# Mixer masks taken in pairs of groups, an fp32 output projection moved by seven steps, and the MLP's transposes one token tile later

## The chip, the cores and the metric

One core of one Trainium2 chip runs the whole program in one launch. The metric is the device time of a launch in microseconds (us), lower is better. TensorE (PE; PEld is its weight load), VectorE (DVE), ScalarE (ACT), GpSimd (POOL) and SyncE (SP, which issues the DMAs) each run their own queue in order and meet at semaphores only.

## The reference, cut to what matters

The input x is 8 sequences x 1024 tokens x 256 features. Three stages follow one another: a Mamba-2 mixer, an MLP (together the "attention" half of a modulated block), and a feed-forward network that the change does not touch.

```
h  = layernorm(x) * (1 + ca) + sa
xn = layernorm(h) * ln_w + ln_b
z, xBC, dt = split(xn @ in_proj_w);  dt = softplus(dt + dt_bias)
x_, B, C   = split(silu(causal_conv1d(xBC)))          # 32 heads of 16, state size 128
state_t = exp(dt*A) * state_(t-1) + dt*x_t (outer) B_t;   y_t = C_t . state_t + D*x_t
y  = y * silu(z)
y  = y * rsqrt(mean(y*y) + 1e-5) * rms_w
o1 = y @ out_proj_w + h                               # mixer
x1 = x + ga * (o1 + relu(layernorm(o1) @ m1 + b1) @ m2 + b2)   # MLP
x  = x1 + gb * feed_forward(layernorm(x1) * (1 + cb) + sb)
```

## The kernel before, in words

**Blocks, chunks, steps.** The mixer works in 16 blocks of 512 tokens, each of 4 chunks of 128 tokens. The scan inside a chunk is a masked product: for every head a 128x128 matrix exp(decay from token s to token t), times the product of B and C (gm), times x. The 32 heads go in 8 groups of 4, so a chunk has 8 steps i = 0..7 and a block 32 steps n = 0..31. Each engine's program is one loop over all steps S = 8q + i (q the chunk); "n" counts from a block's first chunk. While the chunks of one block are scanned, the next block's input side (transposes, input projection, convolution, softplus chain, layer norms) is spread over the same 32 steps by hand: the constants at lines 136 to 156 name the step of each part.

**What a group passes through.** In step S, PE makes group S's decay exponents in a PSUM bank (`decay`, L658), ACT takes exp into a buffer mh (`exponent`, L803), and DVE multiplies the 512 columns by gm (`masked`, L1094). PE uses the result LAG = 5 steps later (`intra`, L672): four fp32 products of 128x32 weights with 128 columns, each placed on 32 of the array's columns by `tile_position`. Heads 2k and 2k+1 add into the same 32 rows of PSUM, so a group of four consecutive heads uses two of the four column tiles, two heads each. There are MH = 7 buffers mh.

**The end of a chunk Q.** DVE's `addends` (step 8Q+9) waits for the last `intra` (PE, step 8Q+12), adds the skip term (L1104) and forms the state's part (yoff_s, L1112). POOL's `gated` (step 8Q+10) adds the two (L907) and multiplies by silu(z) (L914) into yg. ACT (step 8Q+17) makes yh, yg rounded to fp32r (L865), and the square ysq (L866); POOL (step 8Q+16) makes the rest yl = yg - yh (`y_low`, L918). PE (`project`, step 8Q+23) forms yh*wout0 + yh*wout1 + yl*wout0 in twelve one-pass fp32r products of 256 columns (L691, recorded at L645), then the sum of squares with a one-column product (L695). DVE takes the mean (`square_mean`, step 8Q+21, L1119), POOL the power -1/2 (L899), and DVE scales and adds the residual (`residual`, step 8Q+22, L1127). The engines are several steps apart, so such numbers order the work of one engine; they are not times.

**The state.** In i = 1 PE reads the old state (`from_state`, L703), in i = 2 it makes the chunk's contribution (`to_state`, L709, one fp32 product of 512 columns); DVE's `new_state` (i = 0 of the next chunk, L1140 and L1143) waits for it.

**Rings and queues.** PSUM banks are handed round in two rings of three, in the orders that `act_bank_order` and `dve_bank_order` write out (a slot is free again three keys later). SP's queue sends the decay rows (`decay_left`, `decay_right`), stores each finished block (o1) after its last `residual`, and loads the next one.

**The MLP.** 16 blocks of 512 tokens. PE makes eight hidden tiles (m = 0..7), then the second product for the four token tiles c = 0..3: first over the hidden parts k = 0..5 for all c (18 products of 256 columns per c), then k = 6, 7. The transposes of the next block's normalised input go in between (L1310, called at L1346): half k = 0 after c = 0 and half k = 1 after c = 1. They share one PSUM bank: the second waits until ACT has read the first (L1357, L1358). DVE normalises the next block (L1411) after hidden part m = 7, and makes the low part of the transposed input (L1417), with which the next block's products start.

## Time and profile before

| | before |
|---|---|
| median of 3 runs | 3296.01 us (3295.22 to 3304.86) |
| profiled execution | 3288.03 us, span of its instructions 3286.2 us |
| mean granted TensorE clock | 0.941 of 2.4 GHz |
| busy over the span | PE 88%, PEld 67%, DVE 61%, ACT 38%, POOL 24% |
| stages by the trace | set-up to 137 us, mixer to 1421, change of stage to 1449, MLP to 1892, feed-forward to the end |

The busy shares are means over three stages with different limits, so each stage is read by itself: first its busy times by window, then the groups of instructions with the idle time before them and what ended it, then the timeline where the waits lie. A group's "mean ns" is the length of a record; matmuls overlap, so the time that one costs is the distance from its start to the next one's. PE's fp32 products appear as two records each, the one-pass products as one.

### The profile page before, as it was taken

To read this page: it belongs to the slowest core of one execution; us is meant where nothing else is said; L and a number is where in the kernel's file an instruction comes from. 1 tells how busy PE (TensorE), PEld (TensorE's weight loads), DVE (VectorE), ACT (ScalarE), POOL (GpSimd) and SP (SyncE) were. 2 spreads that over 40 slices of the span, in tenths; PEclk is the share of its full clock that TensorE was granted. 3 is DMA by queue.
4 is the path that set the end of the run, shared out by engine and by line. 5 is a ranking of instruction groups with operands and counts; after the bars stand their busy time and mean duration, and the time that the engine had idled before them with its cause. 6 is when DMAs were issued, how large, how long until landed. Compare 5 with 4: busy or idle time off the path is not lost. (4 is left out here: it accounts for less than half of the span.)

```text
span 3286.2 us, 46643 instructions
## 1 busy us (share of the span) xinstructions
PE 2893.6 (88%) x17254; PEld 2215.8 (67%) x17254; DVE 2002.8 (61%) x3954; ACT 1257.5 (38%) x1978; POOL 782.2 (24%) x748
## 2 busy tenths in 40 slices
PE   0588888888888888969988979999999999999999
PEld 0355555555555555558877868787878787878787
DVE  5799989999999999855666533333333333333333
ACT  0455555555555555534555422222222222222221
POOL 5033233333333333320000022222222222222222
PEclk6799989999998999989989989999999999999999
DMA  3000101010101010034211100000000000000000
GB/s 121 28 27 19 34 19 34 20 34 20 34 19 34 19 34 10 28 106 176 73 62 60 47 21 14 16 13 16 13 16 13 15 14 15 13 16 13 15 10 11
DMA packets 104860, 107.11 MB, mean 33 GB/s; under 512 B 35896, under 2 KB 98616, under 8 KB 102976
## 3 DMA queue, kind: packets, MB, share of 16 engines
q1 hardware_dynamic: 99520, 103.81, 9.7%
q8 instruction: 159, 2.61, 0.3%
q10 hardware_dynamic: 5120, 0.19, 0.1%
q14 instruction: 61, 0.50, 0.0%
HBM read 71.41 MB, written 40.94 MB: 34 GB/s over the span
## 5 line engine op out<-in xcount | busy, mean ns | idle before, releaser
L1575 PE MATMUL fbank<-hid,fw 128*128 128x512 f32 x4096 | 962.3, 395 | 0.0
L1575 PEld LDWEIGHTS fbank<-hid,fw 128*128 128x128 f32 x4096 | 765.7, 187 | 187.4
L1725 DVE TENSOR_TENSOR hid<-fhf,hid 128x512 fp32r<-128x512 f32 x384 | 265.4, 691 | 704.4 <-POOL hid L1682 704.4
L803 ACT ACTIVATE mh<-ebank 128x512 f32<-128x512 f32 x512 | 302.8, 601 | 587.9 <-PE ebank L658 587.1
L1682 POOL TENSOR_SCALAR hid<-fhf 128x512 fp32r<-128x512 f32 x384 | 270.6, 705 | 1044.3 <-ACT fhf L1654 760.7
L672 PE MATMUL yin<-mh,xpad 128*32 128x128 f32 x4096 | 345.6, 291 | 104.0 <-DVE mh L1094 102.9
L1094 DVE SCALAR_TENSOR_TENSOR mh<-mh,gm 128x512 f32<-128x512 f32 x512 | 397.0, 782 | 3.1 <-ACT mh L803 3.0
L672 PEld LDWEIGHTS yin<-mh,xpad 128*32 128x32 f32 x4096 | 198.1, 113 | 269.1 <-DVE mh L1094 146.4
L645 PE MATMUL ebank<-ah,win 128*128 128x512 f32 x640 | 246.5, 425 | 6.7 <-DVE al L988 3.6
L1042 DVE SCALAR_TENSOR_TENSOR xc<-cin,cw,xc 128x512 f32<-128x512 f32 x288 | 240.9, 837 | 0.3
L1654 ACT ACTIVATE fhf<-fbank,sh2c 128x512 f32<-128x512 f32 x128 | 88.0, 687 | 382.5 <-PE fbank L1575 382.5
L1598 PE MATMUL fbank<-fah,fw 128*128 128x512 f32 x512 | 205.1, 401 | 16.3 <-issue 12.5
L658 PE MATMUL ebank<-cright,cleft 102*128 102x512 bf16 x512 | 208.2, 407 | 8.6 <-ACT ecs L858 4.3
L1654 ACT ACTIVATE fhf<-fbank,sh1c 128x512 f32<-128x512 f32 x128 | 88.0, 688 | 320.8 <-PE fbank L1575 320.7
L1315 PE MATMUL macc<-wm,mhh 128*128 128x256 f32 x1024 | 202.0, 298 | 3.7 <-DVE mhl L1430 2.7
L1598 PE MATMUL fbank<-fal,fw 128*128 128x512 f32 x512 | 203.6, 398 | 0.0
L1645 ACT ACTIVATE sa<-fbank,s1c 128x512 f32<-128x512 f32 x128 | 88.2, 690 | 264.1 <-PE fbank L1598 241.8
L1315 PEld LDWEIGHTS macc<-wm,mhh 128*128 128x128 f32 x1024 | 170.3, 203 | 7.7 <-DVE mhl L1430 6.2
L899 POOL TENSOR_TENSOR rms<-ms,neg_half 128x1 f32<-128x1 f32 x64 | 88.3, 1380 | 336.7 <-DVE ms L1119 336.7
L1315 PE MATMUL mtile<-mah,wm 128*128 128x512 f32 x512 | 165.3, 398 | 1.0 <-DVE mal L1417 1.0
L907 POOL TENSOR_TENSOR yg<-yin_s,yoff_s 128x512 f32<-128x512 f32 x56 | 90.8, 1621 | 314.3 <-DVE yoff_s L1112 314.3
L645 PEld LDWEIGHTS ebank<-ah,win 128*128 128x128 f32 x640 | 122.6, 192 | 41.5 <-DVE al L988 9.7
(183 smaller groups left out, 4644.3 us busy)
## 6 DMA issues: line engine op xcount, KB each, us to landing
fx<-x_d SPq DMA_DIRECT2D x17, 512.0 KB, 3.9
xs<-in_x SPq DMA_DIRECT2D x16, 512.0 KB, 4.4
h_d<-in_h SPq DMA_DIRECT2D x16, 512.0 KB, 5.2
o_d<-o SPq DMA_DIRECT2D x16, 512.0 KB, 3.1
mo<-o_d SPq DMA_DIRECT2D x16, 512.0 KB, 3.8
mx<-in_x SPq DMA_DIRECT2D x16, 512.0 KB, 4.8
x_d<-mx SPq DMA_DIRECT2D x16, 512.0 KB, 2.8
fw<-h_d SPq DMA_DIRECT2D x2, 4096.0 KB, 14.9
```

What stands on the lines that cost most here:

```text
L645: mm = pe.matmul(o, left[a], right[c], start=(first and n == 0), stop=(last and n == 2))
L658: pe.matmul(fresh(key)[:], cleft[q // NC % 2][:, q % NC, :], cright[q % 2][:, G4 * i:G4 * (i + 1), :].rearrange("k h t -> k (h t)"), start ...
L672: mm = pe.matmul(yin[q % 2][row:row + 2 * HD, h // HQ, :], xpad[q % 2][:, h // 2, h % 2, :, :].rearrange("s w d -> s (w d)"), mh[h_mh.slot ...
L803: nc.scalar.activation(mh[h_mh.slot((q, i))][:].rearrange("s h t -> s (h t)"), tile(key)[:], ACT.Exp).then_inc(free(key), 1)
L1042: ins = dve.scalar_tensor_tensor(out=xc[j % 2][:, m, :], in0=cin[:, m, t:t + HALF], scalar=cw[:, m, t:t + 1], in1=xc[j % 2][:, m, :], op0= ...
L1094: dve.scalar_tensor_tensor(out=m_[:], in0=m_[:], scalar=1.0, in1=gm[q % 2][:].unsqueeze(1).to_broadcast([P, G4, P]), op0=ALU.min, op1=ALU. ...
L1315: mm = pe.matmul(o, left[i], right[j], start=(first and t == 0), stop=(last and t == 2))
L1575: mm = pe.matmul(bank[banks.slot(key)][:], w[:, k, m * P:(m + 1) * P].bitcast(dt), h[:, k, :].bitcast(dt), start=(k + n == 0), stop=(k == ...
L1598: mm = pe.matmul(bank[banks.slot(key)][:], w[:, k, m * P:(m + 1) * P].bitcast(dt), h[:, k, :].bitcast(dt), start=(k + n == 0), stop=(k == ...
L1654: nc.scalar.activation(hf[j % 3][:], bank[banks.slot(key)][:], ACT.Gelu, scale=s[:, m:m + 1]).then_inc(banks.free(key), 1)
L1682: pool.tensor_scalar(hid[i % 2][0][:, m, :], hf[j % 3][:], 1.0, 0.0, ALU.mult, ALU.add)\
L1725: dve.tensor_tensor(hid[i % 2][1][:, m, :], hf[j % 3][:], hid[i % 2][0][:, m, :].bitcast(F32), ALU.subtract).then_inc(c_lo.sem, 1)
```

## The change

- **Pairs.** DVE masks two groups in one instruction of 1024 columns, in odd steps only; mh has four buffers of two groups (MH = 8), handed over in pairs. LAG becomes 6.
- **Head order.** Within a pair of groups, the even group takes heads 0, 2, 4, 6 of the eight and the odd group heads 1, 3, 5, 7. A group's four products therefore go to four different column tiles, one head each; the odd group adds to what the even one began.
- **Projection.** yh and yl are gone. PE forms yg*wout in four fp32 products of 256 columns, straight after yg. It moves from step 8Q+23 to 8Q+16, ACT's square from 8Q+17 to 8Q+16, DVE's mean and residual from 8Q+21 and 8Q+22 to 8Q+14 and 8Q+15, and POOL's power with them. The key "op" stands first in a chunk's part of `dve_bank_order`.
- **SP.** The store of a finished block is queued ahead of the next `decay_left`.
- **Set-up.** The output weights are scaled into one fp32 tensor instead of being split in two (two DVE passes of 1024 columns fewer).
- **MLP.** The two halves of the next block's transposes come after c = 1 and c = 2.

```diff
-LAG = 5
-MH = 7
+LAG = 6
+MH = 8
...
-LAST = (CHUNKS + 2) * NG
+LAST = (CHUNKS + 1) * NG + 1
...
+        if i == 0 and has_chunk(q - 2):
+            yield ("op", q - 2)
...
-        if i == 7 and has_chunk(q - 2):
-            yield ("op", q - 2)
...
-    wout = [sb(f"wout{j}", [P, QI, D], F32R) for j in range(2)]
+    wout = sb("wout", [P, QI, D])
...
-    groups = [(q, i) for q in chunks for i in range(NG)]
...
-    h_mh = Handover(sem, "mh", groups, MH)
+    h_mh = Handover(sem, "mh", [(q, i) for q in chunks for i in range(NG // 2)], MH // 2, uses=2)
...
-    c_yh = Count(sem, "y_hi_made", 0)
-    c_yl = Count(sem, "y_lo_made", 0)
...
-                  (g["w_out"].rearrange("(k p) n -> p k n", p=P), wout, QI, D),
+                  (g["w_out"].rearrange("(k p) n -> p k n", p=P), None, QI, D),
...
-                        last = dve.tensor_scalar(w[:, q, :], w[:, q, :], rmsw[:, q:q + 1], None, ALU.mult)
-                    last.then_inc(s_const, 1)
-                    dve.wait_ge(s_const, 2)
+                        last = dve.tensor_scalar(wout[:, q, :], w[:, q, :], rmsw[:, q:q + 1], None, ALU.mult)
+                    last.then_inc(s_split, 2)
+                    continue
...
-    mh = [sb(f"mh{j}", [P, G4, P]) for j in range(MH)]
+    mh = [sb(f"mh{j}", [P, 2, G4, P]) for j in range(MH // 2)]
...
-    yh = sb("yh", [P, QI, P], F32R)
-    yl = sb("yl", [P, QI, P], F32R)
...
-                if i + 1 < BLOCKS:
-                    decay_left(i + 1)
-                decay_right(NC * i + 3)
...
+                if i + 1 < BLOCKS:
+                    decay_left(i + 1)
+                decay_right(NC * i + 3)
...
-                          cright[q % 2][:, G4 * i:G4 * (i + 1), :].rearrange("k h t -> k (h t)"),
-                          start=True, stop=True).then_inc(full(key), 1)
+                          cright[q % 2][:, i // 2 * HQ + i % 2:(i // 2 + 1) * HQ:2, :], start=True, stop=True)\
+                    .then_inc(full(key), 1)
...
             def intra(q, i):
-                key = (q, i)
+                key = (q, i // 2)
...
-                    h = G4 * i + j
-                    row = HD * 2 * (h % HQ // 2)
-                    mm = pe.matmul(yin[q % 2][row:row + 2 * HD, h // HQ, :],
-                                   xpad[q % 2][:, h // 2, h % 2, :, :].rearrange("s w d -> s (w d)"),
-                                   mh[h_mh.slot(key)][:, j, :], start=(h % 2 == 0), stop=(h % 2 == 1),
+                    row = HD * 2 * j
+                    mm = pe.matmul(yin[q % 2][row:row + 2 * HD, i // 2, :],
+                                   xpad[q % 2][:, G4 * (i // 2) + j, i % 2, :, :].rearrange("s w d -> s (w d)"),
+                                   mh[h_mh.slot(key)][:, i % 2, j, :], start=(i % 2 == 0), stop=(i % 2 == 1),
...
             def project(q):
...
-                pe.wait_ge(c_yl.sem, c_yl.at(0, q + 1))
+                pe.wait_ge(c_yg.sem, c_yg.at(0, q + 1))
...
-                    product(o[:, 0:D], [y[:, f, :] for y in (yh, yl)], [w[:, f, :] for w in wout],
-                            f == 0, f == QI - 1)
+                    pe.matmul(o[:, 0:D], yg[:, f, :], wout[:, f, :], start=(f == 0), stop=(f == QI - 1))
...
+                if i == 0 and has_chunk(q - 2):
+                    project(q - 2)
...
-                if i == 7 and has_chunk(q - 2):
-                    project(q - 2)
...
             def exponent(q, i):
...
-                act.wait_ge(h_mh.free((q, i)), h_mh.used_before(0, (q, i)))
-                nc.scalar.activation(mh[h_mh.slot((q, i))][:].rearrange("s h t -> s (h t)"), tile(key)[:],
+                pair = (q, i // 2)
+                act.wait_ge(h_mh.free(pair), h_mh.used_before(0, pair))
+                nc.scalar.activation(mh[h_mh.slot(pair)][:, i % 2].rearrange("s h t -> s (h t)"), tile(key)[:],
...
-                nc.scalar.activation(yh[:], yg[:], ACT.Copy).then_inc(c_yh.sem, 1)
...
-                if i == 1 and has_chunk(q - 2):
+                if i == 0 and has_chunk(q - 2):
...
             def gated(q):
...
-                    pool.wait_ge(c_ysq.sem, c_ysq.at(0, q))
-                    pool.wait_ge(c_yl.sem, c_yl.at(0, q))
+                    made(pool, ("op", q - 1))
...
-            def y_low(q):
-                pool.wait_ge(c_yh.sem, c_yh.at(0, q + 1))
-                pool.tensor_tensor(yl[:], yg[:], yh[:].bitcast(F32), ALU.subtract).then_inc(c_yl.sem, 1)
...
-                if i == 0 and has_chunk(q - 2):
-                    y_low(q - 2)
...
-                if i == 5 and has_chunk(q - 2):
-                    rms_power(q - 2)
+                if i == 6 and has_chunk(q - 1):
+                    rms_power(q - 1)
...
             def masked(q, i):
-                key = (q, i)
-                if i == 0:
+                key = (q, i // 2)
+                if i == 1:
...
+                released(dve, ("eb", q, i - 1))
...
-                m_ = mh[h_mh.slot(key)]
-                dve.scalar_tensor_tensor(out=m_[:], in0=m_[:], scalar=1.0,
-                                         in1=gm[q % 2][:].unsqueeze(1).to_broadcast([P, G4, P]),
+                m_ = mh[h_mh.slot(key)][:].rearrange("s g h t -> s (g h) t")
+                dve.scalar_tensor_tensor(out=m_, in0=m_, scalar=1.0,
+                                         in1=gm[q % 2][:].unsqueeze(1).to_broadcast([P, 2 * G4, P]),
...
             def addends(q):
-                last = (q, NG - 1)
+                last = (q, NG // 2 - 1)
...
-                if has_chunk(q):
+                if i % 2 and has_chunk(q):
...
-                if i == 5 and has_chunk(q - 2):
-                    square_mean(q - 2)
-                if i == 6 and has_chunk(q - 2):
-                    residual(q - 2)
+                if i == 6 and has_chunk(q - 1):
+                    square_mean(q - 1)
+                if i == 7 and has_chunk(q - 1):
+                    residual(q - 1)
...
-                        if ks[0] == 0 and c < KD and n + 1 < MLP_BLOCKS:
-                            transposes(n + 1, c)
+                        if ks[0] == 0 and 1 <= c <= KD and n + 1 < MLP_BLOCKS:
+                            transposes(n + 1, c - 1)
```

## Rows read from the trace of the kernel before

**Rows 1.** Busy time by window; columns: length, PE, PEld, DVE, ACT, POOL, PEclk, DMA
```profile
137.00:1421.00 1284.00, 1109.86 (x8374) 730.12 (x8376) 1179.57 (x2432) 676.75 (x1128) 400.03 (x279) 0.93 0.09 26
214.00:1371.50 1157.50, 994.15 (x7455) 656.10 (x7455) 1064.66 (x2200) 609.05 (x1015) 356.19 (x250) 0.93 0.09 26
1471.00:1863.00 392.00, 355.19 (x2147) 319.00 (x2148) 237.57 (x510) 202.01 (x326) 19.46 (x14) 0.94 0.24 86
```

**Rows 2.** Groups of instructions in the fourteen middle blocks of the mixer, 214 to 1371.5 us
```profile
L1094 DVE SCALAR_TENSOR_TENSOR mh<-mh,gm 128x512 f32<-128x512 f32 x450 | 346.4, 775 | 3.0 <-ACT mh L803 3.0
L672 PE MATMUL yin<-mh,xpad 128*32 128x128 f32 x3584 | 304.0, 292 | 100.2 <-DVE mh L1094 99.0
...
L918 POOL TENSOR_TENSOR yl<-yg,yh 128x512 fp32r<-128x512 f32 x56 | 75.6, 1350 | 38.2 <-ACT yh L865 38.2
...
L1104 DVE SCALAR_TENSOR_TENSOR yin_s<-xc,dsk,yin 128x128 f32<-128x128 f32 x224 | 62.7, 342 | 26.8 <-PE yin L672 26.4
...
L961 DVE TENSOR_SCALAR nrm<-res,mv,rstd 128x256 f32<-128x256 f32 x52 | 43.6, 897 | 0.0
...
L1140 DVE TENSOR_TENSOR state<-state,dec 128x512 f32<-128x512 f32 x42 | 28.7, 684 | 27.0 <-PE bank L709 27.0
...
L961 DVE TENSOR_SCALAR res<-xs,mv,rstd 128x256 f32<-128x256 f32 x52 | 17.9, 406 | 0.0
...
L976 DVE TENSOR_TENSOR res<-res,shsc 128x1024 f32<-128x1024 f32 x13 | 15.8, 1216 | 0.0
```

**Rows 3.** Timeline around the end of a block: DVE, and PE's wait
```profile
869.61 0.68 DVE L1094 SCALAR_TENSOR_TENSOR mh<-mh,gm 128x512 f32<-128x512 f32 x1
870.21 3.35 DVE L961 TENSOR_SCALAR nrm<-res,mv,rstd 128x256 f32<-128x256 f32 x4
...
880.52 0.66 PE L736 MATMUL ebank<-ident,nrm 128*128 128x128 f32 x4 [1.22 <-ACT ah L811]
...
883.06 0.69 DVE L1140 TENSOR_TENSOR state<-state,dec 128x512 f32<-128x512 f32 x1 [2.18 <-PE bank L709]
```

**Rows 4.** Waits in the MLP stage: waiting engine, releaser, us in total, times, longest
```profile
PE mfront L1310 <- DVE mnrm L1411: 34.1, 15, 2.5
```

**Rows 5.** Timeline of PE at the MLP's transposes, in two of its blocks
```profile
1606.53 0.66 PE L1310 MATMUL mfront<-ident,mnrm 128*128 128x128 f32 x4 [2.50 <-DVE mnrm L1411]
...
1609.15 0.60 PE L1310 MATMUL mfront<-ident,mnrm 128*128 128x128 f32 x4
...
1662.06 1.12 PE L1310 MATMUL mfront<-ident,mnrm 128*128 128x128 f32 x4 [2.49 <-DVE mnrm L1411]
...
1666.81 0.68 PE L1310 MATMUL mfront<-ident,mnrm 128*128 128x128 f32 x4
```

**Rows 6.** Timeline of DVE and POOL around one low half of y
```profile
817.40 1.28 POOL L918 TENSOR_TENSOR yl<-yg,yh 128x512 fp32r<-128x512 f32 x1 [1.33 <-ACT yh L865]
...
817.55 1.28 DVE L1008 SCALAR_TENSOR_TENSOR dser<-dser,dsq 128x128 f32<-128x128 f32 x1
```

**Rows 7.** Timeline of PE; columns: start us, length us, engine, line, operation
```profile
802.74 0.67 PE L745 MATMUL ebank<-af,wdt 128*32 128x128 f32 x16 [0.47 <-ACT ah L811]
803.34 0.39 PE L658 MATMUL ebank<-cright,cleft 102*128 102x512 bf16 x1
803.66 0.64 PE L672 MATMUL yin<-mh,xpad 128*32 128x128 f32 x8
804.23 0.39 PE L658 MATMUL ebank<-cright,cleft 102*128 102x512 bf16 x1
...
810.35 0.51 PE L645 MATMUL bank<-wout,yh 128*128 128x256 f32 x2
...
811.84 0.94 PE L695 MATMUL bank<-ones,ysq 128*128 128x1 f32 x8
...
818.76 1.12 PE L709 MATMUL bank<-xw,bt 128*128 128x512 f32 x2
819.72 0.38 PE L658 MATMUL ebank<-cright,cleft 102*128 102x512 bf16 x1
```

## The prediction, made before any run of the changed kernel

> **What bounds the kernel now.** First the busy times by stage [rows 1]. In the mixer DVE is busy for 1180 of 1284 us and PE for 1110; in the fourteen middle blocks, 82.7 us each, DVE works 76.0 us and PE 71.0. Neither has much slack: DVE sets the pace, with PE five microseconds behind. The MLP belongs to PE (355 of 392 us, clock 0.94). The change leaves the third stage alone.
>
> Second, what the mixer's idle times wait for [rows 2]. PE idles 99 us (7.1 per block) for DVE's masks. DVE idles 53.8 us (3.8 per block) for PE: 27.0 for the state (L1140), 26.8 for the last group of a chunk (L1104). The timeline puts those at one place, the first steps of a block [rows 3]: DVE waits 2.18 us for the state, and PE itself had waited 1.22 us for ACT's input transform (`affine`). So a block has a long stretch bound by DVE and a short one, from about n = 26 to n = 1, bound by PE and ACT.
>
> Third, the MLP: PE waits 34.1 us in 15 pieces for the normalised input [rows 4]. After such a wait of 2.5 us the time from the first to the second set of transposes is 2.62 us in one block and 4.75 in another [rows 5]: there PE ran at the lower of its two clock levels (1.2 for 2.4 GHz).
>
> **The change, part by part.** The sum is made against the profiled execution, 3288.0 us; the median of the runs shown is 8 us (0.24%) above it.
>
> *Pairs.* One pass of 512 columns costs DVE 0.60 us from start to start (869.61 to 870.21 [rows 3]) for a record of 0.68. A record of 1024 columns lasts 1.216 where one of 512 lasts 0.684 [rows 2], so the second 512 cost 0.53: a pair saves 0.07 us. Thirteen of a block's sixteen pairs lie in the DVE stretch: 0.9 us per block. Bounds: nothing, and 0.25 (the masks' mean of 0.775 over 0.53) times 16.
>
> *No low half of y.* What it frees is not POOL but DVE. DVE's 128x128 pass at 817.55 lasts 1.28 us, exactly as long as POOL's yl beside it [rows 6], while 0.68 is enough for one four times as wide. The same normalising pass of 256 columns takes 0.897 us where POOL's gating runs beside it and 0.406 elsewhere [rows 2]. So some DVE passes stand while a POOL pass runs. The cost of a yl to DVE lies between nothing and its whole length, 1.35 us [rows 2]; the masks' mean of 0.775 against 0.68 says that many passes go unhurt, and I take half, 0.64. Three of a block's four count (the fourth falls on DVE's idle time at the block's end): 1.9 us per block. The Trainium skill ("SBUF — State Buffer", SBUF: two separate sides) has a rule on this: a DVE pass with two SBUF inputs and a GpSimd pass exclude each other for the whole of an instruction, whoever starts first. It also speaks against the change, since a pair would shut POOL out for twice as long; the trace agrees as far as rows 6 go.
>
> *Head order.* A group of eight records costs PE 0.57 us (803.66 to 804.23), and the sixteen records of L745 cost 0.60 (802.74 to 803.34) [rows 7]. The first group spreads over two column tiles, the second over four, and both have four records to a tile. So the time goes with the records per tile, and the tiles work side by side: about 0.11 us a record and 0.13 to fill. With four tiles and two records each a group should cost 0.35. That takes 0.22 x 32 = 7 us per block from PE. Nearly all of it falls where PE waits for DVE anyway; it counts at the block's end. Bounds: nothing, and a rise (third rival). The Trainium skill ("TensorEngine Tiling (Array Packing)", Key Properties) says that tiles operate independently and that only a change of the tiling mode drains the array; by that rule the 0.35 would hold, and rows 7 agree.
>
> *Projection.* Twelve one-pass products take 1.49 us (810.35 to 811.84); the fp32 product of 512 columns takes 0.96 (818.76 to 819.72) [rows 7], so four of 256 take 1.92: +0.4 us per chunk on PE, 1.7 per block, covered by the 7 us just freed. If that cover fails, it is 1.7 x 16 = 27 us. ACT loses yh, 0.5 us or so.
>
> *The new places, at the block's end.* Here a mask of groups 26 and 27 must wait for the normalising passes between them. Before, mask 26 ended at 870.2, and the state was there at 883.06, 12.9 us later [rows 3]. Now normalising starts 0.6 us earlier, at 869.6, takes its 3.3 us (still beside POOL's gating), and the pair ends at 874.0. From there PE has the same chain with one decay and intra fewer (0.9), three intras at 0.22 less (0.7), without the 1.22 us wait (ACT no longer has yh and the square ahead of `affine`), and with about 1.2 us less at the low clock: 8.9 us, so the state comes at 882.9, as now. The addends then wait for PE's step n = 5 instead of 4, one decay and intra more at 0.67: +0.7 to +1.2; I take +0.9 us per block. Elsewhere the same longer distance is covered: between a chunk's last pair and its addends DVE has the state's two passes (1.3, from 0.684 each [rows 2]) and a pair (1.13), against two intras and a decay of PE, 1.0 us.
>
> *Other waits and queues.* POOL's power and the residual keep their distance of one step with a longer pass between: nothing. SP's store moves ahead of the next `decay_left`, which waits for a later DVE step anyway: nothing; its cover is the six steps until the decay rows are used. PE's x transposes now need the bank of the projection one chunk back, free after the residual: within 1 us, beside two intras: nothing. In set-up two passes of up to 1.22 us [rows 2] fall away, tail included: 1 us, between 0 and 3.
>
> *MLP.* One token tile is 18 products; 2.62 us less about 0.45 for the transposes is 2.2 us at full clock [rows 5]. Each wait (mean 2.27, longest 2.5) shrinks by up to that: twelve of them, at about 2.5, leave 0.3 each, so 34.1 - 3.6 = 30.5 us. With the waits the low clock goes: up to 2.1 us per block [rows 5]. The granted clock of 0.94 means 23.5 us lost of 392 [rows 1], some inside the waits; I take 18. Next in line is the low half of the transposed input: after the second transposes (0.6 us [rows 5]) it takes two ACT passes and one of DVE of 512 columns, at 0.6 to 0.9 each, some 3 us; PE has one tile (2.2 us) and the 24 products for k = 6, 7 (2.9 at the same rate), 5.1 us. Together 48 us; bounds 28 and 54.
>
> **Sum.** Mixer: 16 x (-0.9 - 1.9 + 0.9) = -30. MLP -48. Set-up and tail -2. 3288 - 80 = 3208 us.
>
> **The rivals.** *First, PE's relief counts more.* If four tiles halve a group's time, the whole block end moves up and most of DVE's 3.8 us there go, and no +0.9 is paid: 16 x 3.9 = 62 us more, 3146. For it: PE is the bound exactly there. Against it: the pair comes 3.8 us later than mask 26 did. *Second, the block's end eats the mixer's gain.* After the transposes of x PE has nothing to do for some 3 us before the pair of 26 and 27, as the projection no longer fills that time; a clock fallen to the low level there makes the projection 3.8 us instead of 1.9. Another 1.9 us per block cancels the 30: 3238. For it: rows 5 show the drop after a wait of 2.5 us. *Third, slower: the head order backfires.* If a change of tile makes each head wait for the one before, a group costs four record lengths of 0.292 [rows 2], 1.17 us instead of 0.57: +19 us per block on PE, of which its 7.1 us of waiting for DVE take the first part. From 71.0 + 19 + 4.6 (PE's other waits) a block lasts 94.9, +12: 3288 + 195 - 50 = 3433. It decides from 0.89 us a group, where it cancels the rest. Against it: L745 changes tile too, and runs four tiles in the time of two. *Fourth, the MLP's wait only moves* to the input transform, a tile later: 3208 + 48 = 3256. Against it: the 5.1 against 3 us.
>
> **How the numbers follow.** Forecast 0.60, first rival 0.14, second 0.19, third 0.04, fourth 0.03. The range runs from the first rival's 3146 to the fourth's 3256, rounded to 3145 and 3256; beyond it lie the third and the tails, under 0.2. A measurement here tells about 0.3% (10 us) from no change. Faster by more: 0.93; same 0.03; slower 0.04.
>
> **What would show it.** Masks 256 records of about 1.22 us with few much longer; intra 0.35 us from start to start; projection 1.9; no L918. PE idle before the MLP's transposes under 10 us and that stage's clock near 1.0. Blocks of the mixer about 80.8 us, with DVE's wait before the addends (L1104) grown and its wait for the state as now. It would be wrong if intra stayed at 0.57 or above 0.89, if DVE's idle time for PE passed 6 us a block, or if ACT's `affine` took over PE's wait in the MLP.

## The result, and the profile after

The changed kernel takes 3213.83 us (median of 4 runs, 3212.33 to 3217.52), the kernel before 3297.23 us in the same session: a ratio of 0.9745, 95% interval 0.9726 to 0.9763. 3208 was forecast. The profiled execution took 3214.82 us, with a span of 3213.1, 73.1 us less than before. By stage (cut at DVE's first pass over the addends of chunks 3, 59 and 63, at PE's first transposes of the MLP and of the third stage; before, then after):

| stretch | before | after | difference |
|---|---|---|---|
| set-up and first block, to 220.3 | 220.3 | 220.3 | 0 |
| mixer, 14 blocks | 1155.7 | 1117.6 | -38.1 |
| mixer, last block | 47.1 | 64.4 | +17.3 |
| change of stage | 26.5 | 25.0 | -1.5 |
| MLP | 461.0 | 409.7 | -51.3 |
| third stage | 1375.6 | 1376.1 | +0.5 |

So the mixer with the change of stage gave 22.3 us where 30 was forecast, in an unexpected way: more per block, and 17 us back in the last one.

Busy times by window, for [rows 1] (fourteen blocks, the MLP's fifteen steady gaps, the last block); columns as there:

```profile
219.00:1336.80 1117.80, 936.08 (x7224) 568.29 (x7223) 997.04 (x1975) 581.64 (x956) 276.78 (x194) 0.89 0.09 26
1450.00:1791.00 341.00, 334.06 (x2141) 298.99 (x2140) 237.18 (x508) 201.62 (x326) 19.43 (x14) 1.00 0.28 99
...
1338.00:1402.00 64.00, 50.27 (x417) 31.96 (x416) 38.63 (x64) 20.11 (x34) 20.35 (x12) 0.81 0.03 10
```

A block takes 79.84 us (1117.8 / 14), of which DVE works 71.2 and waits 8.6; before, 82.68, 76.0 and 6.6 [rows 1]. DVE lost 4.8 us of work and took on 2.0 of waiting. The MLP runs at full clock (1.00, before 0.94 [rows 1]).

The groups for [rows 2], in 219 to 1336.8 us:

```profile
L1081 DVE SCALAR_TENSOR_TENSOR mh<-mh,gm 128x1024 f32<-128x1024 f32 x225 | 275.2, 1223 | 3.4 <-ACT mh L797 3.4
...
L1091 DVE SCALAR_TENSOR_TENSOR yin_s<-xc,dsk,yin 128x128 f32<-128x128 f32 x224 | 62.7, 342 | 30.7 <-PE yin L666 28.4
...
L1127 DVE TENSOR_TENSOR state<-state,dec 128x512 f32<-128x512 f32 x42 | 28.9, 688 | 18.6 <-PE bank L702 18.6
...
L1106 DVE TENSOR_SCALAR ms<-bank 128x1 f32<-128x1 f32 x56 | 8.5, 153 | 41.0 <-PE bank L688 41.0
...
L666 PE MATMUL yin<-mh,xpad 128*32 128x128 f32 x3592 | 203.6, 301 | 54.2 <-DVE mh L1081 54.0
```

Hardly a mask is held up (1223 ns against 1216 for an undisturbed pass of this width [rows 2]; the mean of 775 before was 91 above 684). PE's intra products fell from 304 to 204 us busy, its wait for masks from 99 to 54. The state's wait fell from 27.0 to 18.6 and the addends' rose from 26.8 to 30.7. New is the wait of the first pass that reads the projection's bank, for the mean of squares (L1106): 41.0 us, 2.9 per block, in one place. It was not in the prediction. With it DVE waits 88.0 us for PE (28.4, 18.6 and 41.0), 6.3 a block where it was 3.8.

The timeline around a block's end, where [rows 3] stood (DVE, PE, POOL):

```profile
844.06 3.35 DVE L947 TENSOR_SCALAR nrm<-res,mv,rstd 128x256 f32<-128x256 f32 x4
847.33 1.21 DVE L1081 SCALAR_TENSOR_TENSOR mh<-mh,gm 128x1024 f32<-128x1024 f32 x1
...
853.79 0.16 DVE L1106 TENSOR_SCALAR ms<-bank 128x1 f32<-128x1 f32 x1 [2.46 <-PE bank L688]
...
858.82 0.69 DVE L1127 TENSOR_TENSOR state<-state,dec 128x512 f32<-128x512 f32 x1 [2.79 <-PE bank L702]
...
862.07 1.12 DVE L1091 SCALAR_TENSOR_TENSOR yin_s<-xc,dsk,yin 128x128 f32<-128x128 f32 x4
...
848.59 0.66 PE L666 MATMUL yin<-mh,xpad 128*32 128x128 f32 x8 [1.95 <-DVE mh L1081]
849.18 3.78 PE L685 MATMUL bank<-wout,yg 128*128 128x256 f32 x8
...
845.66 1.27 POOL L906 TENSOR_TENSOR yg<-yg,sz 128x512 f32<-128x512 f32 x1
```

POOL's gating, and with it the projection's input, is done at 846.93. The projection starts only at 849.18, since PE's order has the intra of group 26 ahead of it, and its pair waits behind the normalising passes until 848.5. Then it takes 3.78 us: PE's clock is at its lower level, 1.2 GHz (0.50), and comes back in the course of it:

```profile
844.00:848.50 4.50, 2.45 (x13) 0.94 (x13) 4.50 (x7) 1.71 (x3) 2.58 (x2) 0.50 0.00 1
848.50:851.00 2.50, 2.41 (x12) 1.71 (x13) 2.50 (x7) 0.00 (x0) 0.00 (x0) 0.50 0.79 272
851.00:854.00 3.00, 3.00 (x17) 2.59 (x16) 0.54 (x3) 0.00 (x0) 0.00 (x0) 0.69 0.99 305
854.00:860.00 6.00, 4.98 (x50) 2.64 (x50) 2.73 (x4) 4.53 (x8) 1.48 (x1) 1.00 0.21 65
```

The last block has no next block to prepare, so DVE has little work and the chain is bare: gating, projection, mean. PE comes to the projection seven steps earlier than before, when the gating has not ended. In one of its chunks (POOL, PE, DVE), with this block's window in the kernel before:

```profile
1357.10 2.14 POOL L899 TENSOR_TENSOR yg<-yin_s,yoff_s 128x512 f32<-128x512 f32 x1 [7.83 <-DVE yin_s L1091]
...
1360.63 3.03 PE L685 MATMUL bank<-wout,yg 128*128 128x256 f32 x8 [1.80 <-POOL yg L906]
...
1365.19 0.16 DVE L1106 TENSOR_SCALAR ms<-bank 128x1 f32<-128x1 f32 x1 [3.54 <-PE bank L688]
```

```profile
1376.00:1423.00 47.00, 45.48 (x439) 30.48 (x438) 44.10 (x80) 22.44 (x39) 23.43 (x16) 1.00 0.04 14
```

PE waits for the gating, and its granted clock is 0.81 in this block's window, where it was 1.00. The first two chunks take 17.4 us each where they took 12.4. The gating pass itself lasts 2.14 us beside a mask of a pair. How much of the 17.3 us belongs to which part was not tested one by one, but the experiments bear on it: with single masks the block lasts 55.1 us, and with the projection ahead of the intra products 67.5.

In the MLP, the waits and one block's transposes, for [rows 4, 5]:

```profile
PE mfront L1297 <- DVE mnrm L1398: 4.1, 11, 0.4
```

```profile
1545.15 0.66 PE L1297 MATMUL mfront<-ident,mnrm 128*128 128x128 f32 x4 [0.37 <-DVE mnrm L1398]
1547.77 0.60 PE L1297 MATMUL mfront<-ident,mnrm 128*128 128x128 f32 x4
```

30.0 us of waiting are gone, and the clock granted over the fifteen gaps is 1.00.

### The profile page after: what moved, and what is told of

It is laid out like the page before. It is cut to its first block and busy times, and to the rows that moved or that the text cites. A ratio compares the mean times of both kernels' runs of the same rounds, so it can differ in the third digit from the quotient of the medians.

```text
span 3213.1 us, 45866 instructions
## 1 busy us (share of the span) xinstructions
PE 2820.3 (88%) x16998; PEld 2107.6 (66%) x16998; DVE 1924.4 (60%) x3696; ACT 1228.1 (38%) x1914; POOL 692.6 (22%) x684
## 5 line engine op out<-in xcount | busy, mean ns | idle before, releaser
L1081 DVE SCALAR_TENSOR_TENSOR mh<-mh,gm 128x1024 f32<-128x1024 f32 x256 | 316.2, 1236 | 3.4 <-ACT mh L797 3.4
L666 PE MATMUL yin<-mh,xpad 128*32 128x128 f32 x4096 | 231.6, 301 | 60.2 <-DVE mh L1081 60.0
L1028 DVE SCALAR_TENSOR_TENSOR xc<-cin,cw,xc 128x512 f32<-128x512 f32 x288 | 228.0, 792 | 0.8
L666 PEld LDWEIGHTS yin<-mh,xpad 128*32 128x32 f32 x4096 | 83.6, 111 | 219.5 <-issue 140.0
L1302 PE MATMUL macc<-wm,mhh 128*128 128x256 f32 x1024 | 187.1, 283 | 2.8 <-DVE mhl L1417 1.6
L892 POOL TENSOR_TENSOR rms<-ms,neg_half 128x1 f32<-128x1 f32 x64 | 75.4, 1177 | 452.1 <-DVE ms L1106 452.1
L685 PE MATMUL bank<-wout,yg 128*128 128x256 f32 x512 | 160.5, 468 | 12.9 <-POOL yg L906 12.9
L1302 PEld LDWEIGHTS macc<-wm,mhh 128*128 128x128 f32 x1024 | 157.3, 188 | 6.5 <-DVE mhl L1417 5.1
```

The source lines that it names most:

```text
L666: mm = pe.matmul(yin[q % 2][row:row + 2 * HD, i // 2, :], xpad[q % 2][:, G4 * (i // 2) + j, i % 2, :, :].rearrange("s w d -> s (w d)"), mh ...
L1028: ins = dve.scalar_tensor_tensor(out=xc[j % 2][:, m, :], in0=cin[:, m, t:t + HALF], scalar=cw[:, m, t:t + 1], in1=xc[j % 2][:, m, :], op0= ...
L1081: dve.scalar_tensor_tensor(out=m_, in0=m_, scalar=1.0, in1=gm[q % 2][:].unsqueeze(1).to_broadcast([P, 2 * G4, P]), op0=ALU.min, op1=ALU.mu ...
L1302: mm = pe.matmul(o, left[i], right[j], start=(first and t == 0), stop=(last and t == 2))
```

## The experiments

Twelve kernels ran. Ratios are to the kernel before, run beside each. The block is the mean of the fourteen middle ones; DVE's waiting is the block less DVE's busy time in the window of those blocks. These three columns come from the one profiled execution, which can lie some 10 us from the median (run 2: 3293.88 us, run 3: 3238.75, run 7: 3196.41).

| kernel | median us | ratio (95%) | block | DVE works | DVE waits |
|---|---|---|---|---|---|
| before | 3297.23 | | 82.68 | 76.0 | 6.6 |
| changed | 3213.83 | 0.9745 (0.9726 to 0.9763) | 79.84 | 71.2 | 8.6 |
| 1 MLP alone | 3243.84 | 0.984 (0.9824 to 0.9857) | 83.07 | 76.0 | 7.0 |
| 2 head order alone | 3282.55 | 0.9959 (0.9944 to 0.9974) | 82.73 | 75.2 | 7.6 |
| 3 old head order | 3229.85 | 0.9809 (0.9772 to 0.9846) | 81.63 | 71.3 | 10.4 |
| 4 idle POOL pass | 3244.41 | 0.9867 (0.9845 to 0.9889) | 82.51 | 72.8 | 9.7 |
| 5 single masks | 3179.99 | 0.9648 (0.9632 to 0.9665) | 78.39 | 72.0 | 6.3 |
| 6 normalising at 27 | 3182.82 | 0.9653 (0.9637 to 0.967) | 78.14 | 70.3 | 7.9 |
| 7 both 5 and 6 | 3206.18 | 0.9722 (0.9708 to 0.9735) | 79.59 | 71.3 | 8.3 |
| 8 single, five groups | 3228.05 | 0.9812 (0.9786 to 0.9837) | 81.74 | 73.1 | 8.6 |
| 9 8 and 6 | 3218.9 | 0.9763 (0.975 to 0.9776) | 81.00 | 72.2 | 8.8 |
| 10 projection first | 3184.06 | 0.9641 (0.9619 to 0.9663) | 77.76 | 71.0 | 6.8 |
| 11 5, idle transposes | 3203.58 | 0.9714 (0.9701 to 0.9727) | 78.27 | 72.0 | 6.2 |
| 12 6, idle transposes | 3210.39 | 0.9738 (0.9722 to 0.9754) | 77.93 | 70.3 | 7.6 |

**1. The MLP's part alone**, on the kernel before.

```diff
-                        if ks[0] == 0 and c < KD and n + 1 < MLP_BLOCKS:
-                            transposes(n + 1, c)
+                        if ks[0] == 0 and 1 <= c <= KD and n + 1 < MLP_BLOCKS:
+                            transposes(n + 1, c - 1)
```

> The kernel before with the MLP's transposes one token tile later and nothing else. If this part is worth what its waits and the low clock cost, independently of the mixer: 47 us less than before (3250 us for a run of 3297), PE's wait before the transposes 4 to 6 us instead of 34, that stage's blocks 24.4 us, the mixer unchanged at 82.7 us per block. Rival: part of the 46.6 us that the MLP lost in the changed kernel came with the mixer's end; then less than 40 us.

Measured: 51 us faster. In the profiled execution the MLP stage takes 411.2 us for 461.0, and the mixer's blocks are 0.4 us longer than in the kernel before. So the MLP's gain does not need the rest of the change, and is a little above the 48.

**2 and 3. The head order**, added alone to the kernel before (2), and taken out of the changed kernel (3). In 3:

```diff
-                          cright[q % 2][:, i // 2 * HQ + i % 2:(i // 2 + 1) * HQ:2, :], start=True, stop=True)
+                          cright[q % 2][:, G4 * i:G4 * (i + 1), :].rearrange("k h t -> k (h t)"),
...
-                    row = HD * 2 * j
+                    h = G4 * i + j
+                    row = HD * 2 * (h % HQ // 2)
...
```

> The kernel before with the new head order alone (single masks, LAG 5). If PE's time for a group is the records per column tile: 0.40 us a group instead of 0.57, as in the changed kernel. If it pays only where PE is the bound (a block's end), 1 to 2 us per block, 15 to 30 us in all; if PE was never the bound, under 5 us; if two engines at nearly equal load pass on all of it, 5.4 us per block, 85 us.

> The changed kernel with the old head order (pairs stay). A group should cost 0.57 us again. If the relief matters at the block's end alone, seven groups of 0.17 there: 1.2 us per block and 20 us slower than the changed kernel, with DVE's waits for PE up from 6.5 to about 8 us per block. Rival: the change lives on this relief; then 50 us and more slower.

A group costs 0.36 us from its start to the next product's, not the 0.40 that the expectation gives (changed kernel):

```profile
1370.24 0.43 PE L666 MATMUL yin<-mh,xpad 128*32 128x128 f32 x8
1370.60 0.39 PE L653 MATMUL ebank<-cright,cleft 102*128 102x512 bf16 x1
```

Measured: 13 us faster alone, just under the range of 15 to 30. Without it the changed kernel is some 21 us slower (0.9809 - 0.9745 = 0.0064), but run 3 spreads widely: by the two intervals it is 8 to 34 us. Alone most of it turned into PE's waiting, as the row of its waits for masks shows (99.0 us before [rows 2]):

```profile
PE yin L671 <- DVE mh L1093: 119.8, 86, 2.7
```

In run 3 DVE waits for PE 8.4 us a block, in the changed kernel 6.3; most of the rise is in the wait before the addends, 3.5 for 2.0. That the order counts more once DVE's load is cut is not shown, as the two intervals overlap.

**4. A POOL pass put back.** One pass of 512 columns per chunk, on constants, where nobody waits for it, in the changed kernel.

```diff
+            def idle_pass(q):
+                pool.wait_ge(c_ysq.sem, c_ysq.at(0, q + 1))
+                v = ones[:].unsqueeze(1).to_broadcast([P, QI, P])
+                pool.tensor_tensor(yx[:], v, v, ALU.subtract)
...
+                if i == 0 and has_chunk(q - 2):
+                    idle_pass(q - 2)
```

> The changed kernel with one POOL pass of 128x512 added per chunk, after the square, at the place of the old yl; its result is used by nobody. If what the missing yl gave was DVE's freedom from POOL's passes: DVE's busy time up by 0.5 to 0.7 us per chunk (2 to 2.7 us per block, among them records of about 2 us), 25 to 40 us slower. Rival: POOL passes hurt DVE only where they meet certain passes, and here the place holds none: under 8 us. If the yl pass explains all of the 4.8 us per block by which DVE's busy time fell, less 1.1 for the pairs, 3.7 us per block come back.

Measured: 31 us slower by the medians, 40 by the ratios, for a pass that nobody reads; 2.7 us per block, 0.67 per pass. The row of the pass and one of DVE's that it holds (0.688 without it):

```profile
L912 POOL TENSOR_TENSOR yx<-ones 128x512 f32<-128x512 f32 x56 | 81.4, 1454 | 0.0
...
L1135 DVE TENSOR_TENSOR state<-state,dec 128x512 f32<-128x512 f32 x42 | 34.7, 826 | 33.0 <-PE bank L703 33.0
```

DVE's work grows by 1.6 us per block and its waits by 1.1. So the 2.7 us that the pass takes from a block are nearly what the whole change gave it (2.8): POOL's absence is the larger part of the mixer's gain, as the prediction said. Of the 4.8 us by which DVE's work fell, 1.6 come back here and the pairs explain 1.0 (runs 6 and 7); no run assigns the rest.

**5. Single masks** of 512 columns in the changed kernel, still six groups behind, eight buffers.

```diff
-                key = (q, i // 2)
+                key = (q, i)
...
-                                         in1=gm[q % 2][:].unsqueeze(1).to_broadcast([P, 2 * G4, P]),
+                                         in1=gm[q % 2][:].unsqueeze(1).to_broadcast([P, G4, P]),
...
-                if i % 2 and has_chunk(q):
+                if has_chunk(q):
                     masked(q, i)
...
```

> The changed kernel with 512 masks of 512 columns instead of 256 of 1024, LAG 6 and eight buffers. If a pair only saves the fixed cost: DVE's busy time up 1.1 us per block (16 x 0.07), but mask 26 no longer waits for the normalising passes, so up to 2 us per block come back at the block's end: about equal to the changed kernel, within 15 us either way. Rival: single masks in even steps meet POOL's gating again; then DVE's busy time rises by 2 to 3 us per block and the kernel is 15 to 40 us slower.

Measured: 34 us **faster** than the changed kernel, in neither of the expected ranges, though DVE works 0.8 us per block more. Its waits in the fourteen blocks:

```profile
DVE yin_s L1090 <- PE yin L666: 34.3, 14, 5.6
DVE state L1126 <- PE bank L702: 18.3, 7, 2.8
...
PE yin L666 <- DVE mh L1080: 10.8, 17, 1.1
...
DVE ms L1105 <- PE bank L688: 3.8, 1, 3.8
```

The wait for the mean is gone (3.8 for 41.0), PE's wait for masks nearly. The last block is shorter too: 55.1 us by the table's marks, for 64.4.

**6. Normalising one step later**, pairs kept: mask pair 26/27 goes before the last normalising passes.

```diff
-LN_AT = (18, 20, 21, 22, 24, 26)
+LN_AT = (18, 20, 21, 22, 24, 27)
```

> The changed kernel with the last part of the layer norm (the four normalising passes) one step later, n = 27 instead of 26, behind the pair of groups 26 and 27. If DVE's new wait before the mean (2.9 us per block) comes from that pair being 3.3 us late, with PE idle before it and then at the low clock: the pair ends 3 us earlier, the wait falls below 1 us, 1.5 to 2.5 us per block, 25 to 40 us faster. Rival: the chain of the next block's transposes (normalise, transpose, ACT, transpose) holds the block's end; then later normalising gives nothing or costs up to 1 us per block (15 us).

Measured: 31 us faster than the changed kernel, about as much as without pairs, but not by the expected sign alone. DVE's wait for the mean was to fall under 1 us a block; it fell from 2.9 to 1.9. The normalising passes, no longer beside POOL's gating, got shorter (first the changed kernel's row, then run 6's and its wait for the mean):

```profile
L947 DVE TENSOR_SCALAR nrm<-res,mv,rstd 128x256 f32<-128x256 f32 x52 | 43.6, 898 | 0.0
```

```profile
L947 DVE TENSOR_SCALAR nrm<-res,mv,rstd 128x256 f32<-128x256 f32 x52 | 31.4, 663 | 0.0
```

```profile
DVE ms L1106 <- PE bank L688: 26.6, 15, 4.1
```

That is 0.9 us of DVE's work a block, over half of the 1.7 gained. Over the twelve middle blocks the mean does come sooner, 8.72 us after the start of DVE's yoff_s pass instead of 10.67, but DVE, with less work, is there sooner too. So this run moves two things at once, the mask's place and the meeting with the gating, and doesn't tell them apart; run 10 does.

**7. Both together.**

> The changed kernel with both single masks and the last normalising step at n = 27. Each of the two took 31 to 34 us from the changed kernel. Theory A (both cured one and the same thing, mask 26 held behind the normalising passes and with it the wait for the mean): together they give little more than one alone: 3170 to 3185 us, ratio to before 0.962 to 0.966, the wait for the mean under 0.3 us a block. Theory B (the single masks gain by a shorter distance to PE everywhere, the normalising step by the place alone, so they add up): 3145 to 3160 us, ratio 0.954 to 0.959. Theory C (pairs do save DVE's time once the place is cured, 0.07 us a pair, 0.9 us a block): with single masks here the mixer's block is 0.9 us longer than with the pairs and the step at n = 27 (78.14 us), 79.0 us and 3195 us.

Measured: 3206 us, outside the ranges of A and B, and C is nearest. DVE's wait for the mean is 22.4 us, 1.6 a block, where A had under 0.3. Against run 6 DVE works 1.0 us per block more: that is the price of singles, 0.06 us a pair, and nearly what the prediction had. Against run 5 the kernel is 24 us slower by the ratios: masks 26 and 27 now stand beside POOL's first gating pass, which takes longer:

```profile
838.05 2.20 POOL L899 TENSOR_TENSOR yg<-yin_s,yoff_s 128x512 f32<-128x512 f32 x1 [0.88 <-DVE yin_s L1090]
```

It takes 1.60 us in run 5 and 1.31 in the changed kernel. Over twelve middle blocks the gating ends 3.76 us after the start of DVE's yoff_s pass in run 5, 4.36 in run 7, and the mean comes after 8.58 and 9.14.

**8. Single masks, five groups behind**, with seven buffers; the diff is against run 5.

```diff
-LAG = 6
-MH = 8
+LAG = 5
+MH = 7
```

> The changed kernel with single masks, seven buffers and the scan products five groups behind the decay, as in the kernel before, the other parts of the change left in. Theory A (the sixth group of distance costs at the block's end what the prediction said, one decay and one intra more before the addends, 0.7 to 1.2 us a block, and elsewhere nothing): against single masks with six groups (3180 us) 11 to 19 us faster, 3161 to 3169, with the wait before the addends down from 2.45 us a block to about 1.5. Theory B (the sixth group gives PE slack against masks that come late behind DVE's other passes, and costs nothing): with five groups PE waits more for masks and the kernel is slower, 3185 to 3210. Theory C (no effect): 3175 to 3185.

Measured: 48 us slower than run 5 (54 by the ratios), B's direction and more than its range. The distance and the number of buffers moved together, and no run separates them. The waits:

```profile
PE yin L666 <- DVE mh L1080: 117.1, 110, 2.5
...
DVE ms L1105 <- PE bank L688: 27.1, 14, 3.7
```

PE waits for masks eleven times as long (117.1 for 10.8), and the mean is late again. With five groups the intra ahead of the projection is that of group 27, whose mask comes after the normalising: the projection starts 5.79 us after the start of the yoff_s pass (the same twelve blocks), as in the changed kernel (5.73), not after 3.84.

**9. The same with normalising at 27.**

> The run with single masks five groups behind (0.9812), now with the last normalising step at n = 27. With five groups PE has the intra of group 27 ahead of the projection, and mask 27 stood behind the normalising passes, so the projection started 5.8 us after DVE's yoff_s pass began. Theory A (that wait made the run with five groups slow): it now starts at 4.4 us, and the kernel is 1.4 to 2 us a block faster, 22 to 35 us: ratio 0.970 to 0.975. Theory B (five groups cost mainly by PE's waits for masks in the middle of the block, 8.4 us a block against 0.8): the gain is under 10 us, ratio 0.978 or more. Theory C (five groups now save the last step before the addends as well): 0.960 to 0.965.

Measured: 9 us faster than run 8 (by the ratios 0.5%, 16 us), between A and B. The projection starts at 4.42 us and the mean comes at 9.32 for 10.46, but PE still waits 87.6 us for masks, where run 7, with the same step for the normalising and six groups, has 10.4:

```profile
PE yin L666 <- DVE mh L1080: 87.6, 95, 2.3
```

```profile
PE yin L666 <- DVE mh L1080: 10.4, 15, 1.1
```

Yet run 9 is only 13 us slower than run 7. So five groups cost 54 us with the normalising at 26 and 13 at 27: PE's 77 us more of waiting for masks cost little, and the greater part of the price comes only together with the normalising ahead of mask 27. How it arises in detail is not shown.

**10. The projection ahead of the intra products** in the changed kernel, nothing else.

```diff
-                if has_chunk((S - LAG) // NG):
-                    intra(*divmod(S - LAG, NG))
                 if i == 0 and has_chunk(q - 2):
                     project(q - 2)
+                if has_chunk((S - LAG) // NG):
+                    intra(*divmod(S - LAG, NG))
```

> The changed kernel with one thing moved on PE: in the first step of a chunk the projection stands ahead of the intra products, not behind them. Everything else, the pairs and the normalising step at n = 26, stays. Theory A (the pair of groups 26 and 27 is held by the normalising passes, the intra of 26 waits for it, and the projection, the mean and all behind it wait in PE's order): the projection starts some 3.6 us after DVE's pass over yoff_s begins, when POOL's gating ends, not after 5.7; DVE's wait for the mean falls from 2.9 us a block to under 1; 25 to 40 us faster than the changed kernel, ratio to before 0.962 to 0.967. Theory B (single masks and the later normalising step gained by something else, such as shorter DVE passes): no change, ratio 0.973 to 0.976.

Measured: 30 us faster than the changed kernel (34 by the ratios), theory A in all its numbers. The block's end (POOL, PE, DVE):

```profile
829.37 1.27 POOL L906 TENSOR_TENSOR yg<-yg,sz 128x512 f32<-128x512 f32 x1
...
830.69 3.78 PE L685 MATMUL bank<-wout,yg 128*128 128x256 f32 x8 [0.33 <-POOL yg L906]
834.26 1.71 PE L688 MATMUL bank<-ones,ysq 128*128 128x1 f32 x8
835.90 0.65 PE L666 MATMUL yin<-mh,xpad 128*32 128x128 f32 x8
...
831.03 1.21 DVE L1081 SCALAR_TENSOR_TENSOR mh<-mh,gm 128x1024 f32<-128x1024 f32 x1
...
836.01 0.16 DVE L1106 TENSOR_SCALAR ms<-bank 128x1 f32<-128x1 f32 x1 [0.97 <-PE bank L688]
```

The projection follows the gating at once, the pair is masked beside it, and the wait for the mean falls to 0.7 us a block (9.4 us in all). DVE's passes are as they were (71.0 us of work a block for 71.2). So this run shows the cause by itself: the projection stood behind the intra products that wait for the held mask. The wait for the state rises to 29.0 us (18.6), and the last block, where the move has nothing to gain, lasts 67.5 us for 64.4.

**11 and 12. Filling PE's idle time** before the block's end with twelve idle transposes, in runs 5 and 6.

```diff
-                if q % NC == 0:
-                    pe.wait_ge(c_xc.sem, c_xc.at(0, q // NC + 1))
...
+                if q % NC == 0:
+                    for _ in range(12 if q else 0):
+                        pe.transpose(o[:, 0:P], ident[:], ident[:])
+                    pe.wait_ge(c_xc.sem, c_xc.at(0, q // NC + 1))
```

> The run with single masks and six groups (0.9648) with twelve idle transposes of the identity on PE in the bank of the next transposes of x, at each block's end, where PE otherwise waits 1.9 to 3.7 us for ACT's gated input. They add 1.3 us of work where PE is idle and change no result. Theory A (the projection at the block's end runs its eight products in 3.4 us on average, not 1.9, since PE's clock fell to the lower level after that idle time): with the idle time filled the projection takes 1.9 to 2.5 us, the mean comes 1 to 1.5 us sooner and the kernel is 10 to 25 us faster, ratio 0.957 to 0.962. Theory B (the low clock there is set by something else, or has no part in the chain): ratio 0.963 to 0.967 with the projection as long as before. Theory C (the transposes delay what follows): slower, 0.967 or more.

> The same twelve idle transposes in the run with pairs and the normalising step at n = 27 (0.9653), whose blocks differ: some have the projection in 2.9 to 3.2 us, others in 3.78, and the mean then comes 1.3 us later. Theory A: projection 1.9 to 2.5 us in all, 10 to 30 us faster, ratio 0.956 to 0.962. Theory B: no change, 0.964 to 0.967.

Measured: 24 and 28 us slower, but not in the mixer: its blocks are 0.1 and 0.2 us shorter (last section). The projection's mean length stayed (3.48 us for 3.43). At the block's end shown here the transposes ran from 820.6 to 823.4 us, at a clock of 0.60 and then 0.55; it was 1.00 from 824 to 826, and with the next wait, of 1.5 us up to 826.7, it fell again (run 11):

```profile
824.00:826.00 2.00, 0.82 (x10) 0.25 (x9) 1.97 (x10) 1.89 (x4) 1.40 (x1) 1.00 0.04 8
826.00:828.00 2.00, 1.26 (x12) 0.59 (x12) 2.00 (x4) 0.28 (x1) 1.19 (x1) 0.80 0.01 4
828.00:830.00 2.00, 1.57 (x18) 0.49 (x11) 2.00 (x3) 1.12 (x3) 1.68 (x2) 0.50 0.00 0
```

So the attempt didn't bring the state about that it was to test. What a projection at full clock would be worth stays open.

## Why the prediction was right, and where not

The time (3208 for 3214) and the sign came out; of the 80 us forecast 73 are in the trace. The MLP agrees with its cause. In the mixer errors cancel: the middle blocks gave more than forecast (38.1 us for 14 x 1.9 = 26.6), the last one lost 17.3, and the block's end went another way than described. That the sum there lies within 8 us of the forecast is luck. One of the prediction's own signs of being wrong came true: DVE's idle time for PE passed 6 us a block, it is 6.3.

- **MLP, -48:** measured -51.3 in the trace and 51 us in run 1. Waits 34.1 to 4.1 (forecast 3.6), clock 1.00. This step held, with its cause.
- **No low half of y, -1.9 per block:** right mechanism, too small in sum. Put back into the changed kernel (run 4) a pass costs 0.67 us, near the 0.64, but four of them cost 2.7 a block: either the fourth, which was to fall on DVE's idle time, is not free, or the others cost more. Run 4's pass reads constants and stands among pairs, so for the kernel before this is the nearest price, not the price itself.
- **Pairs, -0.9:** DVE's work falls by 1.0 us per block (runs 6 and 7) and 0.8 (run 5 and the changed kernel). The term held as DVE's work. As a part of the change, pairs lost 34 us (run 5), by where they stand: run 10 keeps them and loses nothing to run 5.
- **Head order:** a group takes 0.36 us from start to start for the 0.35 forecast and 0.57 before, with four column tiles. That most of PE's 7 us a block would go into waiting for DVE held (run 2: 13 us alone).
- **Projection, +0.4 per chunk, hidden:** the size held at full clock, 1.83 us from its start to the next product's (forecast 1.92; the twelve took 1.49), and a record of 1.99. But at a block's end it runs at 1.2 GHz in 3.78 us, as the second rival had it. It is not hidden there: the mean, the residual, the state and the addends wait behind it.
- **Block's end, +0.9, "the state comes at 882.9, as now":** this is the step that failed. From the end of the yoff_s pass before the normalising (844.06) to the state are 14.8 us, where they were 13.5 (869.61 to 883.06 [rows 3]); +1.3 and not 0. To the addends it is 18.0 for 16.0, so +2.0 where +0.9 stood. The prediction followed intra, state and addends, and did not ask who else stands behind the pair in PE's order: the projection, and DVE's mean behind it. The pair is ready when forecast, 4.5 us after normalising begins (4.4); from there the state takes 10.3 us and not 8.9. "1.2 us less at the low clock" did not come: the granted clock over that way is 0.79, where it was 0.81 from the end of mask 26 to the state, and in the fourteen blocks it is 0.89 for 0.93. Run 10, with the projection moved, gets 2.1 us a block back.
- **"16 x":** the sum took every block alike. The first, with the set-up, gave nothing. In the last one DVE has no other work while PE waits for the gating, and it gave back 17.3 us of the 38.1.

Of the rivals, the second was right about the place and the 3.8 us; its 3238 did not come, since a middle block still fell by 2.7 us. The third (a group above 0.89 us) and the fourth are out. The first (3146) did not come either; even runs 5, 6 and 10 stay at 3180 to 3184 us, and no run tests in them what PE's relief gives.

The best versions of these are the changed kernel with the projection ahead of the intra products, with single masks, or with the normalising at 27: about 1.0% less time than the changed kernel's and 3.5% less than before. The three can't be told apart here, and the projection first together with single masks was not run.

## What to carry to other kernels

Before an operation is made longer or later, list everything behind it in the queue of each engine that waits for it, not only its own readers: here a mask waited for by an early product held the projection that stood behind in PE's order, and moving two lines brought 30 us. A removed pass can be worth most on another engine, so look for passes of equal length that stand side by side. And cost the first and last turn of a loop by themselves, since they lack the work that covers a longer chain.

## What the hardware showed

- A POOL pass that reads constants and that nobody waits for costs 31 to 40 us over 64 passes of 1.45 us (run 4). The Trainium skill ("SBUF — State Buffer", SBUF: two separate sides) says that a GpSimd pass which reads SBUF and a DVE pass with two SBUF inputs, or in a two-port mode, exclude each other for a whole instruction. The traces agree in kind, and it works both ways: beside the normalising passes POOL's gating pass lasts 1.31 us and they are held (four in 3.35 us, where 0.406 is one's undisturbed length [rows 2]); beside the masks of run 7 it lasts 2.20 itself, which then delays PE. The normalising passes have one input, and no run here shows in which mode they run.
- At full clock, groups of eight records took 0.36 us over four column tiles (two records each) and 0.57 over two (four each).
- PE's clock fell without a long wait. In the changed kernel it was 1.00 from 832 to 838 us, where PE was busy for 4.00 of 6.00 us, 0.60 from 838 to 844 (3.03 of 6.00) and 0.50 from 844 to 848.5 (2.45 of 4.50), and none of the waits there is longer than 1.95 us. The eight records of a projection then took 3.78 us together, for 1.99 elsewhere.
- A loop at a distance can pay for added instructions. In runs 11 and 12 the third stage, whose code is the same, took 26 and 24 us more than in runs 5 and 6. PE waits there for its own instructions ("issue") fourteen times instead of seven, in run 5 and then in run 11:

```profile
PE fbank L1584 <- issue: 12.7, 7, 2.0
```

```profile
PE fbank L1586 <- issue: 27.7, 14, 2.5
```

Each of the seven stops became two, the second one two products in (run 11). The products behind it start 0.43 us apart and later 0.23, as they do behind the one stop of run 5:

```profile
2325.77 0.49 PE L1586 MATMUL fbank<-fah,fw 128*128 128x512 f32 x1 [1.75 <-issue]
2326.10 0.39 PE L1586 MATMUL fbank<-fal,fw 128*128 128x512 f32 x1
2328.99 0.55 PE L1586 MATMUL fbank<-fah,fw 128*128 128x512 f32 x1 [2.50 <-issue]
```

In every other run, and in the kernel before, the stage takes 1374.8 to 1378.8 us with seven stops. The number of PE instructions ahead of the loop does not decide it alone: the profile has 10718 matmul records ahead of it in the changed kernel, 10974 in the kernel before, and 10898 in runs 11 and 12. What decides it is open. It means that a difference of some 20 us between kernels with other instruction counts needs a look at the stages before it is put down to the edit.
